# Set-up of a fused tokenizer kernel: weight scaling moved to ScalarE, pooling and first moments moved ahead

## The reference

```python
reduce_feats = x.mean((3, 5))...                  # 4x4 pixels pooled: 16x16 tokens an image
q  = _ln(reduce_feats, ln_q_w, ln_q_b) @ Wq.T     # layer norm over the 64 channels
kv = _ln(unf, ln_kv_w, ln_kv_b) @ Wkv.T           # of every pixel
attn  = softmax(einsum('bhpd,bhpnd->bhpn', q * scale, k))   # 16 pixels of a token, 8 heads
aggre = einsum('bhpn,bhpnd->bhpd', attn, v)
h = reduce_feats + aggre @ proj_w.T + proj_b
```

## Time and profile before

| | us |
|---|---|
| median of 3 runs | 677.42 (676.17 to 678.1) |
| the profiled execution | 676.25 |
| its span (first to last instruction) | 674.5 |
| TensorE matmul busy in the span | 605.5 (90%) |
| VectorE busy | 551.9 (82%) |
| ScalarE busy | 458.8 (68%) |
| GpSimd busy | 455.4 (68%) |

### The profile page before, as it was taken

The page is one execution under the profiler, slowest core; times in us unless marked ns, Lnnn a source line. Parts: engine busy times, 40 slices in busy tenths (PEclk is TensorE's granted clock), DMA queues, the critical chain, the costliest instruction groups (busy, mean ns, idle before and its releaser), DMA issues. The chain is left out here.

```text
span 674.5 us, 16753 instructions
## 1 busy us (share of the span) xinstructions
PE 605.5 (90%) x5386; PEld 331.1 (49%) x5386; DVE 551.9 (82%) x991; ACT 458.8 (68%) x931; POOL 455.4 (68%) x443
## 2 busy tenths in 40 slices
PE   1899999999999999995799999986149999999995
PEld 1223333333333333331356666653048899889884
DVE  4589999999999999988659988888458888888882
ACT  0787777877777787762488888884136677666673
POOL 5756988889898889655621766666705666666666
PEclk9999999999999999998999999999569999999998
DMA  7233333333332222000074951111122222222210
GB/s 293 91 126 126 125 125 126 126 125 125 127 120 93 89 97 104 19 7 8 0 122 96 199 180 36 41 37 41 53 57 60 62 61 58 61 58 59 57 34 1
DMA packets 49213, 57.80 MB, mean 86 GB/s; under 512 B 31986, under 2 KB 44804, under 8 KB 46906
## 3 DMA queue, kind: packets, MB, share of 16 engines
q1 hardware_dynamic: 43738, 48.02, 23.8%
q0 software_dynamic: 5120, 6.84, 3.2%
q10 hardware_dynamic: 288, 2.10, 0.8%
HBM read 50.03 MB, written 10.28 MB: 89 GB/s over the span
## 5 line engine op out<-in xcount | busy, mean ns | idle before, releaser
L1937 POOL DMA_INDIRECT out<-orow,m_rows x96 | 107.5, 1120 | 74.6 <-ACT orow L1882 53.7
L825 PE MATMUL s_proj<-x_px,w_kv 64*64 64x512 f32 x256 | 131.2, 605 | 0.0
L822 PE MATMUL s_proj<-x_px,w_kv 64*64 64x512 f32 x256 | 130.6, 602 | 0.1
L1831 DVE TENSOR_TENSOR m_xs<-m_rows 128x768 f32<-128x768 f32 x96 | 91.5, 954 | 34.3 <-ACT m_rows L1863 15.5
L487 POOL TENSOR_TENSOR half_px<-x_px 128x1024 f32<-128x1024 f32 x30 | 71.6, 2386 | 35.7 <-DMA x_px<-in_x 35.7
L1188 POOL DMA_INDIRECT rows_by_group<-r_pay,r_slot_i x64 | 65.6, 1025 | 43.5 <-ACT r_h L1283 7.3
L508 POOL TENSOR_TENSOR pre<-va 128x1024 f32<-128x1024 f32 x32 | 76.1, 2379 | 26.0 <-DVE va L608 24.3
L590 DVE TENSOR_TENSOR qk<-s_proj,q 128x512 f32<-128x512 f32 x128 | 85.5, 679 | 8.3 <-PE s_proj L825 6.0
L313 ACT ACTIVATE x_sq<-x_px 128x1024 f32<-128x1024 f32 x64 | 67.1, 1048 | 33.4 <-PE b_x L877 19.2
L608 DVE TENSOR_TENSOR va<-b_a,v_sb 128x1024 f32<-128x1024 f32 x64 | 78.1, 1220 | 7.7 <-PE b_a L842 7.7
L1917 PE MATMUL mixed_bank<-m_xsT,m_w_cur 128*64 128x128 f32 x1344 | 84.0, 276 | 0.0
(11 more groups left out here) (281 smaller groups left out, 1726.7 us busy)
## 6 DMA issues: line engine op xcount, KB each, us to landing
x_px<-in_x SPq DMA_DIRECT2D x15, 2048.0 KB, 7.9
m_rows<-rows_by_group SPq DMA_DIRECT2D x96, 72.0 KB, 1.8
wt<-in_w2T SPq DMA_DIRECT2D x8, 512.0 KB
rows_by_group<-rows_by_group SPq DMA_DIRECT2D x1, 2286.0 KB, 10.5
x_px<-in_x ACTq DMA_DIRECT2D x2, 1024.0 KB, 6.4
out<-orow,m_rows POOLq DMA_INDIRECT x96, 2.5
rows_by_group<-r_pay,r_slot_i POOLq DMA_INDIRECT x64
wt<-in_w2T SPq DMA_DIRECT2D x2, 256.0 KB
```

The source lines that it names most:

```text
L822: mm(b_k[i][LO, :], w_kv[LO, 0, LO], px(t, j, LO), start=True, stop=True)
L825: mm(b_k[i][HI, :], w_kv[HI, 0, HI], px(t, j, HI), start=True, stop=True).then_inc(done["kv_product"], 1)
L1831: d.tensor_tensor(xs[:, i % RING, :, :], rows[:, i, X0:X0 + C].rearrange("p (o c) -> p o c", o=1).broadcast_to([P, UNITS, C]), rows[:, i, ...
L1937: nc.gpsimd.indirect_dma_start(out_d, bass.IndirectOffsetOnAxis(ap=rows[:, i, ID0:ID0 + 1].bitcast(I32), axis=0), orow[:, i, :], None, bou ...
```

## The change

It moves and replaces steps of the set-up; no loop of the later tiles changes.

- The three weight scalings go from VectorE to ScalarE, as activations with a per-partition scale, behind its table load and the wait for the small loads. ScalarE's wait for the seven folds goes from ahead of its loop to `q_final(0)`.
- VectorE scales the averaging matrix first, then pools both halves of tile 0, and only then waits for the small loads and the products and copies the folds.
- GpSimd makes the masks in `e_sw` itself: one memset of 128 x 1024, then for each half of the columns two selects over 128 x 512. `MASKS` becomes 33; the moments of the pixels wait for step 28 (`SELECTED`) alone. VectorE's two copies (L242) and the waits for them go.
- On TensorE the bias product (L253) moves from the set-up block to behind `q_moments(0)`, which now waits for the averaging matrix alone (`folded` 1); `kv(0, 0)` waits for the seven folds, the last of which is the bias add that reads bank `b_v[0]`.

```diff
-    LOADS, CENTRED, MASKS, FOLDED, SWAPPED = 16 * 6, 8, 31, 7, 9
+    LOADS, CENTRED, SELECTED, MASKS, FOLDED = 16 * 6, 8, 28, 33, 7
...
-        step(g.memset(e_f[:, :, :], 1.0))
-        band(e_f[:, :, :], 0.0, 0, [[16 * HD, NCH], [1, P]], -HD, HD - 1, [[-16 * HD, NCH], [-1, P]], HD)
+        step(g.memset(e_sw[:, :, :], 1.0))
+        for b in range(2):
+            band(e_sw[:, :, C * b:C * b + C], 0.0, C * (1 - b), [[16 * HD, NCH], [1, C]], -HD, HD - 1 - C * (1 - b), [[-16 * HD, NCH], [-1, C]], HD)
...
-        v.wait_ge(loaded, LOADS)
         v.wait_ge(masks, CENTRED)
-        for i, w in ((0, 0), (1, 2), (2, 2)):
-            nc.vector.tensor_scalar(w_sc[:, i, :], w_ld[:, i, :], vec[:, w:w + 1], None, ALU.mult).then_inc(scaled, 1)
         nc.vector.tensor_scalar(avg_px[:, :], avg[:, :], 1.0 / NP, None, ALU.mult).then_inc(folded, 1)
         v.wait_ge(x_top, 16)
         pool_half(0)
+        v.wait_ge(x_in[0], 16)
+        v.wait_ge(top_pooled, 1)
+        pool_half(1)
+        v.wait_ge(loaded, LOADS)
         v.wait_ge(prod, 1)
...
-        v.wait_ge(x_in[0], 16)
-        v.wait_ge(top_pooled, 1)
-        pool_half(1)
         v.wait_ge(prod, 2)
         nc.vector.tensor_tensor(vec[:, 7:8], b_v[0][:, 0:1], vec[:, 4:5], ALU.add).then_inc(folded, 1)
-        v.wait_ge(masks, MASKS)
-
-        for b in range(2):
-            s, o = slice(C * b, C * b + C), slice(C * (1 - b), C * (1 - b) + C)
-            nc.vector.tensor_copy(e_sw[:, :, s], e_f[:, :, o]).then_inc(folded, 1)
...
-        pe.wait_ge(folded, 6)
-        nc.tensor.matmul(b_v[0][:, 0:1], w_ld[:, 3, :], vec[:, 6:7], start=True, stop=True).then_inc(prod, 1)
...
             act.wait_ge(done["q_scaled"], t + 1)
+            if t == 0:
+                act.wait_ge(folded, FOLDED)
...
         act.preload_act_table_set("natural_log_exp_and_others")
+        act.wait_ge(loaded, LOADS)
+        for i, w in ((0, 0), (1, 2), (2, 2)):
+            a.activation(w_sc[:, i, :], w_ld[:, i, :], ACT.Identity, scale=vec[:, w:w + 1]).then_inc(scaled, 1)
         act.wait_ge(x_top, 16)
         act.wait_ge(zeroed, 3)
-        act.wait_ge(folded, FOLDED)
...
                 if t == 0:
                     pe.wait_ge(x_top, 16)
+                    pe.wait_ge(folded, FOLDED)
...
             if m == 0:
-                pe.wait_ge(folded, SWAPPED)
+                pe.wait_ge(masks, MASKS)
...
             if t == 0:
-                pe.wait_ge(masks, MASKS)
+                pe.wait_ge(masks, SELECTED)
...
             if t == 0:
-                pe.wait_ge(folded, FOLDED)
+                pe.wait_ge(folded, 1)
...
             q_moments(t)
+            if t == 0:
+                pe.wait_ge(folded, 6)
+                mm(b_v[0][:, 0:1], w_ld[:, 3, :], vec[:, 6:7], start=True, stop=True).then_inc(prod, 1)
```

More of the change, by code:

```diff
@@ L128, in tokenizer @@
     msel = sb("msel", [P, 2, 32])
-    e_f = va[:, 0:2, :].rearrange("p a (b m) -> p (a b) m", m=P)
     e_sw = sb("e_sw", [P, NCH, P])
@@ L600, in va_mul @@
             v.wait_ge(done["a_spread"], 4 * t + i + 1)
-            if t == 0 and n == 0:
-                v.wait_ge(folded, SWAPPED)
             if n == 0:
```

## The result

The changed kernel took 673.02 us as the median of 4 runs (671.78 to 673.65) against 677.39 for the kernel before: 4.37 us less, ratio 0.9939 (95% interval 0.9923 to 0.9954). Repeated later it gave 672.59 (median of 6) against 677.36, ratio 0.9925 (0.9909 to 0.9942). The profiled execution took 672.78 us with a span of 671.0.

The account below looks back on a forecast made before the run. TensorE was taken to bound the steady tiles, so the start's gain shifts everything: 0.9 plus 4.7 make 5.57 us, 0.84 lost, 0.4 to 1.3 regained, cut to 5.4, 5.3 taken. Forecast 672.1 us, range 669.8 to 674.8.

Parts of the forecast that it names:

- rival 1: TensorE's clock stays low through the start, not raised by the thin products; 4.7 us arrive, 672.7 us; chance 20%.
- What bounds it: Steady tiles: TensorE busy all 16.80 us, VectorE 15.41; an earlier first tile should shift everything behind it.
- Weights on ScalarE: Start: three scalings take 1.0 us on ScalarE, weights ready at 10.63 instead of 11.52, a gain of 0.9 us.
- Pooling first: Start, VectorE: both halves pooled before the folds; moments' operands ready 1.0 us before TensorE finishes the products.
- Moments ahead of the bias product: Start, TensorE: moments at 13.0, 5.57 us earlier; behind bias and kv products the q product gains only 4.73 us.
- The clock: TensorE's rise from 1.2 to 2.4 GHz in the start chain: gives back 0.4 to 1.3 us.
- if the rise comes as long behind the moments' start as before: In-between clock case: rise falls into the second kv product, shortens its last pass by 0.4; pixel moments 5.1 us earlier.
- The lower bound of 4.7 us: Clock low to the chain's end: pixel moments 2.40 us behind the q product as before, at 19.7 instead of 24.44.
- What is late next: VectorE's pooling of tile 1 waits for GpSimd's part, ready at 24.58: ceiling of 5.4 us on the gain, 5.3 taken.
- Masks: GpSimd's four selects at 0.66 us each end at 12.0, before it is next needed; dropping VectorE's copies is worth nothing.
- Rival 2: Part is swallowed further on, by the mix stage's clock or waits in the first tiles: 673.0 to 675.3 us; chance 13%.
- Rival 4: Slower: VectorE and GpSimd meet differently in steady tiles, VectorE grows past 16.80 us a tile: 680.5 us; chance 5%.

Follow-up runs that it names:

- e9: Kernel before with one part of the change alone, the weight scalings on ScalarE: 676.94 us against 677.19, ratio 0.9995.
- e7: Changed kernel with the pooling of tile 0's bottom half back behind the folds: 676.20 us, ratio 0.9977 to the kernel before.
- e1: Changed kernel with the bias product back in the set-up, ahead of the moments; other chip: 692.77 us, ratio 0.9940 to the kernel before there.
- e2: Changed kernel with the bias product in an unused bank, behind the first pixel moments; other chip: 692.39 us, ratio 0.9937 to the kernel before there.
- e3: Changed kernel with 16 matmuls of unread results on TensorE ahead of the products; other chip: 690.08 us, ratio 0.9898 to the kernel before there.
- e4: Changed kernel with 16 unread matmuls ahead of the products and the bias product in its own bank; other chip: 690.97 us, ratio 0.9922.
- e10: Changed kernel with unread matmuls on TensorE in both gaps, 16 before the products and 44 before the mix: 672.24 us, ratio 0.9919.
- e6: Changed kernel with the masks made as before, by two selects of 1024 elements and VectorE's two copies: 673.41 us, ratio 0.9932.
- e8: Changed kernel with 44 unread matmuls on TensorE while it waits for the mix to begin: 674.06 us, ratio 0.9952 to the kernel before.
- e5: Changed kernel with the three weight scalings back on VectorE, between the poolings of the two halves: 673.11 us, ratio 0.9939.

## Why the prediction came out as it did

The sign was right and the time lay in the range, 5.3 us forecast and 4.4 measured. But 4.4 lies below the gains of 4.9 to 5.7 that the forecast itself named, and the times of 673.02 and 672.59 are nearer to the 672.7 of rival 1, which had 20%, than to 672.1. Two of its signs were missed: pixel moments at 20.23 (18.4 to 19.7) and tile 1 at 25.75 (24.5 to 25.3). In the profiles 5.3 us were forecast at tile 1 and 4.2 came: 0.2 us are missing behind the bias product, 0.9 in the clock.

- *What bounds it*: right, but a tile takes 18.15 us, not the 16.80 of the earlier trace rows, a stretch chosen too short. TensorE is busy for all 18.15 and VectorE for 16.61. A shift of the start goes through the steady tiles unchanged (250.7 us between tiles 1 and 15 in both kernels). That single profiles lose 0.9 to 1.6 us of it behind the tiles was not seen.
- *Weights on ScalarE*: 0.98 us against 1.0; the chain moved by 0.87 (10.70 against 11.57) and e9 shows 0.93. Alone they bring nothing that the time shows.
- *Pooling first*: right in mechanism and size. The moments waited for the products, not for ScalarE (11.90 against 12.93), and e7 puts most of the gain here.
- *Moments ahead of the bias product*: the step by which 5.57 us at the moments become 4.73 at the q product was right in kind: 5.64 and 4.56, so 1.08 us were lost there and not 0.84. The moments held TensorE for 14.83 - 12.93 = 1.90 us, not 1.76, and from the add's end to the kv product passed 0.14, not 0.05. e1 and e2 confirm the mechanism: 0.48 us for the order and 1.1 us for the wait of the first kv product on the add.
- *The clock*: this is the term that failed. The prediction let it give back 0.4 to 1.3 us, by the case "if the rise comes as long behind the moments' start as before". It gave nothing back and took 0.35 (4.56 at the q product, 4.21 at the pixel moments), since the kernel before had the rise inside this chain and the changed one did not. The lower bound of 4.7 us had overlooked that: the 2.40 us from the q product to the pixel moments, taken from the kernel before, held a pass of 0.77; in the changed kernel they were 2.75. Rival 1 named the mechanism: 4.7 by its sum, 4.2 and 3.9 by the profiles. Its reason, the thin products, was not tried by itself.
- *What is late next*: the ceiling at tile 1 is real (e2, e3, e4, e10) but didn't bind in the changed kernel. It is 24.0 to 24.5, by tile 1's landing, rather than 24.6, and 1 us of what it cuts off comes back by tile 2: at tile 15 e10 is 6.5 us ahead of the kernel before, so the ceiling of 5.4 was too low for what lies behind; GpSimd's first halving no longer shares its time with mask copies (2.35 us instead of 2.55).
- *Masks*: 0.66 us each as by the line; worth nothing (e6). The longer selects did no harm that a profile shows.
- *Rival 2*: in single profiles something is indeed swallowed further on, but at the end of the tiles, where the clock falls, and at a scatter's transfer, not in the mix, where e8 found 0.2 us. The medians don't show a loss. *Rival 4*: nothing of it; VectorE is busy for 16.61 us a tile in both kernels, and by its own reckoning would have had to exceed 18.15, not 16.80.

## What to carry to other kernels

Work whose operands are there should stand ahead of work that waits for a load, on every engine of the start; each microsecond that the whole chain gains then passes whole through a steady stage that one engine fills. Before promising more, look for the next input with a time of its own (here tile 1's landing and GpSimd's share), because it cuts off most of what the chain gains beyond it. And a stretch that TensorE spends at its lower level should be priced in both kernels, the one before included: the rise can fall inside the old chain and outside the new one.

## What was not expected of the hardware

The moment at which TensorE's clock rises at the start is not tied to the start of its work by any fixed time. These are the starts of the moments and of the first pass that was shorter than 1.06 us (0.63 for the q product's shape):

| profile | moments start | first pass at a higher clock |
|---|---|---|
| before, and repeated | 18.57, 18.56 | 23.74 (0.77 us), 23.73 (0.91 us) |
| changed, and repeated | 12.93, 12.69 | in the pixel moments from 20.23, from 19.99 (partly) |
| e7 | 16.58 | in the pixel moments from 23.89 (partly) |
| e9 | 17.63 | 20.25 (0.83 us) |
| e5 | 14.06 | 20.32 (0.68 us) |
| e8 | 13.06 | 19.33 (0.92 us) |
| e6 | 13.03 | 18.45 (0.85 us) |
| e1 | 14.28 | 18.60 (0.78 us) |
| e2 | 12.49 | 15.96 (0.50 us) |

Among profiles whose work on TensorE is the same from the moments on, the next kv product behind the pixel moments came 7.73, 7.87 and 6.52 us after the moments' start (before, repeated, e9) and 9.15, 9.83, 9.00 and 8.51 (changed, repeated, e8, e6). So up to 1.3 us of chain hang on it, more than the weights (0.9) or the order (0.5) are worth. It agrees with the Trainium skill, TensorE: Matmul & The Clock Gate (What's actually happening), in that the moment of the change varies between executions. With work without use in the gap ahead there was no such spread (e3, e4, e10, one profile each: every pass of the chain at the full level), and tile 1 was at its ceiling in all three. Only e2 got there without it, in its one profile, where the clock rose at 15.96.
